# Prologue order of a Perceiver layer kernel: small weights and last rows moved into step 0

## The reference

```python
x = x + xattn(layernorm(x), ctx)     # x 64x32x256, ctx 64x257x256
x = x + attn(layernorm(x))
x = x + ffn(layernorm(x))

def xattn(x, y):
    Q = x @ Wq + bq;  K = y @ Wk + bk;  V = y @ Wv + bv
    K_hat = cos(K @ Wr + br)
    return softmax(Q @ K_hat.T) @ V

def attn(x):                          # causal, the 8 most similar earlier tokens
    score = where(top8(x @ x.T), (x @ W_q.T) @ (x @ W_k.T).T / sqrt(32), -1e9)
    msg = softmax(score) @ x
    mix = sigmoid(log_mix);  scale = softplus(log_scale) + 0.01
    return gelu((mix * x + (1 - mix) * msg) * gain + bias) * scale

def ffn(x):                           # one of 8 experts per token, 256 -> 1024 -> 256
    return p_max * (gelu(x @ W1[e] + b1[e]) @ W2[e] + b2[e])
```

## Time and profile before

| | us |
|---|---|
| median of 3 runs | 526.98 (525.98 to 528.96) |
| profiled execution, its own time | 528.04 |
| profiled execution, span of the trace | 526.1 |
| PE busy in the span | 458.0 (87%) |
| DVE, ACT, POOL busy | 272.8, 267.9, 206.6 |

### The profile page before, as it was taken

How to read it: one execution, slowest core, us unless ns; L and a number is a source line. 1 busy time by engine, 2 the same in 40 slices (tenths; PEclk the granted TensorE clock), 3 DMA queues, 4 the chain that set the end, 5 groups by cost and what they waited for, 6 DMA issues and landing times. The chain is left out here.

```text
span 526.1 us, 10389 instructions
## 1 busy us (share of the span) xinstructions
PE 458.0 (87%) x2848; PEld 339.0 (64%) x2849; DVE 272.8 (52%) x794; ACT 267.9 (51%) x580; POOL 206.6 (39%) x377
## 2 busy tenths in 40 slices
PE   4889999999999889999997632169999999999992
PEld 3555555666666456666564421169999999999991
DVE  1456878778787578778776546501222221222110
ACT  2267668877788578777785331023332233322230
POOL 2441235334453155243532210643544455445331
PEclk9999999999999999999997655569999999999997
DMA  8602521435314333263340012466557555566110
GB/s 229 204 30 91 171 91 44 148 112 191 111 50 143 112 107 102 90 190 110 111 162 20 20 41 101 145 234 220 191 209 212 210 162 182 200 219 208 47 21 0
DMA packets 47880, 68.93 MB, mean 131 GB/s; under 512 B 5469, under 2 KB 39839, under 8 KB 47713
## 3 DMA queue, kind: packets, MB, share of 16 engines
q1 hardware_dynamic: 41808, 59.09, 33.9%
q0 software_dynamic: 3312, 8.13, 5.7%
q10 hardware_dynamic: 2720, 1.26, 0.9%
HBM read 62.17 MB, written 7.21 MB: 132 GB/s over the span
## 5 line engine op out<-in xcount | busy, mean ns | idle before, releaser
L1177 PE MATMUL pK<-stage,Wkr 128*128 128x512 f32 x256 | 124.3, 611 | 2.6 <-DVE stage L674 2.0
L340 POOL TENSOR_SCALAR ve<-mv 128x1 f32<-128x1 f32 x48 | 13.7, 286 | 185.5 <-DVE mv L597 185.5
L1369 PE MATMUL b<-W,XF 128*128 x368 | 83.1, 379 | 0.0
L1369 PEld LDWEIGHTS b<-W,XF 128*128 128x128 f32 x368 | 68.2, 190 | 8.4
L1177 PEld LDWEIGHTS pK<-stage,Wkr 128*128 128x128 f32 x256 | 44.5, 193 | 43.0 <-issue 41.7
L964 DVE SCALAR_TENSOR_TENSOR XF<-b,p_slot,XF 128x256 f32<-128x256 f32 x23 | 11.1, 484 | 104.6 <-PE b L1369 104.6
L1015 ACT ACTIVATE stage<-pK,bkr 128x512 f32<-128x512 f32 x64 | 42.8, 689 | 38.1 <-PE pK L1177 38.1
L1110 ACT ACTIVATE XF<-pT,b_now 128x128 f32<-128x128 f32 x96 | 27.3, 370 | 54.4 <-PE pT L1351 54.3
L1110 ACT ACTIVATE XF<-pK,b_now 128x128 f32<-128x128 f32 x88 | 25.2, 369 | 50.6 <-PE pK L1351 50.6
L1022 ACT ACTIVATE stage<-stage 128x512 f32<-128x512 f32 x64 | 40.5, 633 | 14.9 <-DVE stage L669 14.7
L1351 PE MATMUL pT<-XF,stage 128*128 128x128 f32 x384 | 46.6, 282 | 0.0
(11 more groups left out here) (204 smaller groups left out, 762.2 us busy)
## 6 DMA issues: line engine op xcount, KB each, us to landing
stage<-in_L_ffn_W_dram SPq DMA_DIRECT2D x23, 1024.0 KB
stage<-in_ctx_dram SPq DMA_DIRECT2D x32, 512.0 KB, 4.9
W<-in_L_ffn_W_dram SPq DMA_DIRECT2D x8, 1024.0 KB, 6.0
ctx_last<-in_ctx_dram SPq DMA_DIRECT2D x64, 32.0 KB, 3.9
normal_tokens<-xn SPq DMA_DIRECT2D x16, 128.0 KB, 2.9
residual_tokens<-X SPq DMA_DIRECT2D x16, 128.0 KB, 2.7
X<-in_x_dram SPq DMA_DIRECT2D x1, 1792.0 KB, 7.5
stage<-in_L_ffn_b_dram SPq DMA_DIRECT2D x1, 1024.0 KB, 6.6
```

Source lines behind the costliest of these rows:

```text
L1177: mm = pe.matmul(pK[r][:], Wkr[:, c, r * P:(r + 1) * P], ctx_T[:, c, half * 512:(half + 1) * 512], start=c == 0, stop=c == DC - 1)
L1369: mm = pe.matmul(p_out[b], f_hT[b][:, n * P:(n + 1) * P], W2[:, bass.ds(e, 1), n, :].rearrange("p o d -> p (o d)"), start=n == 0, stop=n = ...
```

## The change

- SP: Wr gets a semaphore of its own, `wr_ld`. ACT: bk and br count on `bk_ld`, and the two logs are issued ahead of x and Wqk.
- PE: the first transposes wait for Wk alone. The key bias moves behind the first context transposes of step 0, the transposes of Wqk and of the last rows (now in b7) behind the second projection, the projection of the last rows (now in b4) behind the second half's context transposes. The three waits ahead of step 0 go; a wait for `wkr_cp` stands ahead of the first projection.
- DVE: the scalars come ahead of step 0; the key bias follows the copy of xnT, the two copies stand ahead of `whole(0, 0)`, the operations of the last rows ahead of `whole(0, 2)`.
- ACT: the wait for `bkr_cp` moves ahead of the first `turn`, and the Sin of the last rows behind the last `sine` of step 0.
- POOL: in step 0 it waits for `khat_last` at the end of the step, copies the column, and makes the masks; the gains move to the end of step 1.

```diff
@@ POOL
-            def late_constants():
+            def gains():
                 pool.wait_ge(S["scal_dve"], 3)
                 (gain_msg, gain_self)
+                pool.wait_ge(S["gains"], 2)
+            def masks():
                 (causal, pickable, unpicked)
...
-                if now:
+                first = isinstance(k, int) and 2 * k + parity == 0
+                def last_key():
                     g, b, _ = now
-                    if isinstance(g, int) and g == 0:
-                        pool.wait_ge(S["khat_last_r"], 1)
...
+                if now and not first:
+                    last_key()
...
-                if isinstance(k, int) and 2 * k + parity == 0:
-                    late_constants()
+                if first:
+                    pool.wait_ge(S["khat_last_r"], 1)
+                    last_key()
+                    masks()
+                if isinstance(k, int) and 2 * k + parity == 1:
+                    gains()
@@ DVE
-            (key bias, copies of WqkT and last_T, last rows' turns and fraction)
             normal_x(0, 0)
+            scalars()
...
                     v.tensor_copy(xnT[:].rearrange("p c n -> p (c n)"), p_xnT).then_inc(S["xnT_cp"], 1)
+                    if isinstance(g, int) and g == 0:
+                        key_bias()
...
                 if now:
+                    if isinstance(now[0], int) and now[0] == 0:
+                        early_copies()
                     whole(now[0], 0)
...
                 if now:
+                    if isinstance(now[0], int) and now[0] == 0:
+                        last_keys()
                     whole(now[0], 2)
@@ ACT
-            act.dma_start(bk[:], ...).then_inc(S["wk_ld"], 16)
-            act.dma_start(br[:], ...).then_inc(S["wk_ld"], 16)
+            act.dma_start(bk[:], ...).then_inc(S["bk_ld"], 16)
+            act.dma_start(br[:], ...).then_inc(S["bk_ld"], 16)
+            act.dma_start(logs[:, 0:1], a["L0_attn_log_mix"].partition_broadcast(P)).then_inc(S["logs_ld"], 16)
+            act.dma_start(logs[:, 1:2], a["L0_attn_log_scale"].partition_broadcast(P)).then_inc(S["logs_ld"], 16)
             act.dma_start(X[:, 0:2, :], x_v[:, 0:2, :]).then_inc(S["x_ld"], 16)
...
-            act.wait_ge(S["bkr_cp"], 1)
...
                 if now:
+                    if isinstance(now[0], int) and now[0] == 0:
+                        act.wait_ge(S["bkr_cp"], 1)
                     turn(now[0], 0)
...
                     sine(g, b, 3)
+                    if isinstance(g, int) and g == 0:
+                        last_keys()
@@ PE
-            pe.wait_ge(S["wk_ld"], 64)
+            pe.wait_ge(S["wk_ld"], 16)
...
+            pe.wait_ge(S["wr_ld"], 16)
...
-            pe.wait_ge(S["bkr_cp"], 1)
-            pe.wait_ge(S["wqkT_cp"], 1)
-            pe.wait_ge(S["last_turn"], 2)
...
                     ctx_transposes(g, b, q, 0)
+                    if first:
+                        key_bias()
...
+                if first:
+                    pe.wait_ge(S["wkr_cp"], 1)
                 if now:
                     ctx_project(now[0], 0, 0)
...
                     ctx_project(now[0], 0, 1)
+                if first:
+                    early_transposes()
...
                     ctx_transposes(g, b, q, 1)
+                if first:
+                    last_keys()
```

More of the change, by code:

```diff
@@ new lines, in scalars @@
+            def scalars():
+                v.wait_ge(S["scal_act"], 1)
+                v.tensor_scalar(sc[:, 1:2], sc[:, 0:1], 1.0, None, ALU.add).then_inc(S["scal_dve"], 1)
+                v.wait_ge(S["scal_dve"], 1)
+                v.reciprocal(sc[:, 2:3], sc[:, 1:2]).then_inc(S["scal_dve"], 1)
+                v.wait_ge(S["scal_dve"], 2)
+                v.tensor_scalar(sc[:, 3:4], sc[:, 2:3], -1.0, 1.0, ALU.mult, ALU.add).then_inc(S["scal_dve"], 1)
+                v.tensor_scalar(sc[:, 8:9], logs[:, 1:2], 0.0, 0.01, ALU.max, ALU.add).then_inc(S["scal_dve"], 1)
+                v.wait_ge(S["scal_act"], 4)
+                v.wait_ge(S["scal_dve"], 4)
+                v.tensor_tensor(sc[:, 9:10], sc[:, 7:8], sc[:, 8:9], ALU.add).then_inc(S["scal_dve"], 1)
+                v.wait_ge(S["scal_dve"], 5)
@@ L992, in _, with last_keys, scalars @@
             act.dma_start(Wroute[:], rows(a["L0_ffn_Wr"])).then_inc(S["w_ld"], 16)
[L995 to L1003, removed]
+            def last_keys():
+                act.wait_ge(S["last_fr"], 1)
+                act.activation(khat_last[:], last_frac, ACT.Sin, scale=TWO_PI).then_inc(S["khat_last_r"], 1)
+            def scalars():
+                act.wait_ge(S["logs_ld"], 2 * 16)
+                act.activation(sc[:, 0:1], logs[:, 0:1], ACT.Exp, scale=-1.0).then_inc(S["scal_act"], 1)
+                act.activation(sc[:, 5:6], logs[:, 1:2], ACT.Abs).then_inc(S["scal_act"], 1)
+                act.wait_ge(S["scal_act"], 2)
+                act.activation(sc[:, 6:7], sc[:, 5:6], ACT.Exp, scale=-1.0).then_inc(S["scal_act"], 1)
+                act.wait_ge(S["scal_act"], 3)
+                act.activation(sc[:, 7:8], sc[:, 6:7], ACT.Ln, bias=1.0).then_inc(S["scal_act"], 1)
+            scalars()
             def ctx_T_copy(g, half):
@@ L1136, in _ @@
             mm.then_inc(S["wkr_mm"], 1)
[L1137 to L1145, removed]
@@ L1146, in _ @@
-            pe.wait_ge(S["last_ld"], 16)
-            for c in range(DC):
-                transposed(b7[:, c * B:(c + 1) * B], last_rows[:, c * P:(c + 1) * P],
-                           "lastT_tr" if c == DC - 1 else None)
-            pe.wait_ge(S["wkr_cp"], 1)
-            pe.wait_ge(S["lastT_cp"], 1)
-            for r in range(DC):
-                for c in range(DC):
-                    mm = pe.matmul(b6[:, r * B:(r + 1) * B], Wkr[:, c, r * P:(r + 1) * P], last_T[:, c, :],
-                                   start=c == 0, stop=c == DC - 1)
@@ L1156, in _, with key_bias @@
-            mm.then_inc(S["lastK_mm"], 1)
-            pe.wait_ge(S["bkr_cp"], 1)
-            pe.wait_ge(S["wqkT_cp"], 1)
-            pe.wait_ge(S["last_turn"], 2)
+            def key_bias():
+                pe.wait_ge(S["bk_ld"], 2 * 16)
+                for r in range(DC):
+                    for ec in range(DC):
+                        mm = pe.matmul(b4[:, r:r + 1], Wr[:, ec, r * P:(r + 1) * P], bk[:, ec:ec + 1],
+                                       start=ec == 0, stop=ec == DC - 1)
+                mm.then_inc(S["bkr_mm"], 1)
@@ new lines, in early_transposes @@
+            def early_transposes():
+                pe.wait_ge(S["wqk_ld"], 32)
+                for c in range(DC):
+                    transposed(b7[:, c * 2 * H:(c + 1) * 2 * H], Wqk[:, c * P:(c + 1) * P],
+                               "wqkT_tr" if c == DC - 1 else None)
+                pe.wait_ge(S["last_ld"], 16)
+                for c in range(DC):
+                    transposed(b7[:, P + c * B:P + (c + 1) * B], last_rows[:, c * P:(c + 1) * P],
+                               "lastT_tr" if c == DC - 1 else None)
@@ L1162, in ctx_transposes, with last_keys @@
+            def last_keys():
+                pe.wait_ge(S["lastT_cp"], 1)
+                pe.wait_ge(S["bkr_sum"], 1)
+                for r in range(DC):
+                    for c in range(DC):
+                        mm = pe.matmul(b4[:, P + r * B:P + (r + 1) * B], Wkr[:, c, r * P:(r + 1) * P], last_T[:, c, :],
+                                       start=c == 0, stop=c == DC - 1)
+                mm.then_inc(S["lastK_mm"], 1)
             def ctx_transposes(g, b, q, half):
@@ L1225, in step @@
                     pe.wait_ge(S["hT_cp"], g + 1)
+                    if isinstance(g, int) and g == 0:
+                        pe.wait_ge(S["wqkT_cp"], 1)
                     at_least(pe, S["xnT_cp"], upto(g + 3, NG))
```

62 lines of the change are left out of this document (26 added, 36 removed).

## The result

The changed kernel is slower, by a little. Its median is 530.51 us (529.27 to 531.26, ten runs), beside 527.81 (525.98 to 529.32, ten runs) of the kernel before: a ratio of 1.0049, with a 95% interval of 1.0030 to 1.0068. The forecast was 524.8 with a range of 522.8 to 526.9. The profiled execution of after has 530.77 with a span of 529.0, where before had 528.04 and 526.1.

The account below looks back on a forecast made before the run. PE was taken as the bound, busy 15.57 of 15.65 us of a step. A gain of 5.35 less 1.4 less 1.75 gave 2.2 us off the median of 526.98: 524.8 us, range 522.8 to 526.9.

Parts of the forecast that it names:

- the load of x costs nothing: Prologue: x behind the two logs lands up to 2 us later, at 10.6, but is wanted only at 14.3.
- nothing past step 1 is touched: Later steps: PE bounds each, so a saving ahead of step 3 reaches the end whole; 2.2 us forecast.
- part 1: Prologue up to the first key projection: it starts at 14.9 and not 20.25, a gain of 5.35 us.
- part 2: Step 0, work moved behind the second projection: third projection at 23.6, 3.95 earlier than before, a cost of 1.4 us.
- part 3: After the last sine of step 0: POOL's later masks delay L1245 of step 1, a cost of 1.75 us.
- PE's start, the context load, the biases: Prologue: PE starts at 4.7, the second context load lands at 10.7, the key bias ends at 14.3.
- The moved work: Step 0: small transposes and last rows' projection on PE behind the second projection; third projection at 23.6.
- T: The time in step 0 when the second projection has been issued, forecast at 20.2.
- The table load: ACT's load of the Sin set in step 0: 1.28 us; the skill page's dearer switch, 1.35 longer, had chance 0.03.
- The masks: POOL's masks take 4.65 us (bounds 4.4 to 5.4), delaying rstd(2), DVE's copy of the probabilities and L1245 in step 1.
- Rival (a): Prologue: PE's clock rises early, about 11, first projection at 13.8; 1.7 us more gained, 523.1; chance 0.14.
- Rival (c): Ahead of the scores: PE's clock falls after 2.05 us idle, costing 1.5 to 3.5 us; 524.9 to 526.9; chance 0.17.

Follow-up runs that it names:

- e7: Changed kernel with the load of x issued ahead of the two logs in ACT's queue; 528.24 us, ratio 1.0018 to the kernel before.
- e11: Changed kernel with eight more fulfilled waits on DVE in step 1 and x loaded ahead of the logs; 521.42 us, ratio 0.9867 to the kernel before.
- e3: Changed kernel with POOL's masks ahead of its wait for khat_last in step 0; 529.64 us, ratio 1.0032 to the kernel before.
- e2: Changed kernel with two fulfilled waits on constants left out on DVE in stats_x of groups 3 and 4; 529.03 us, ratio 1.0025 to the kernel before.
- e5: Changed kernel with eight more fulfilled waits on DVE in step 1; 524.82 us, ratio 0.9951 to the kernel before.
- e6: Kernel before with eight more fulfilled waits on DVE in step 1; 522.39 us, ratio 0.9918 to the kernel before.
- e9: Kernel before with four more fulfilled waits on DVE in step 1; 530.13 us, ratio 1.0037 to the kernel before.
- e4: Changed kernel with two more fulfilled waits on DVE in step 1; 529.82 us, ratio 1.0051 to the kernel before.
- e10: Changed kernel with eight more fulfilled DVE waits and POOL's masks ahead of its wait for khat_last; 523.21 us, ratio 0.9898 to the kernel before.
- e8: Changed kernel with x ahead of the logs, POOL's gains and masks ahead of its khat_last wait, and eight more DVE waits; 520.53 us, ratio 0.9883.
- e12: Changed kernel with eight more fulfilled DVE waits and POOL's masks and gains in step 0 ahead of its khat_last wait; 523.06 us, ratio 0.9888.
- e1: Kernel before with two more fulfilled waits on DVE in step 1; 528.52 us, ratio 1.0019 to the kernel before.

## Why the prediction was wrong, step by step

Two steps failed: that the load of x costs nothing, and that nothing past step 1 is touched. In the profiled pair the sum of the prediction reads so: part 1 gained 3.79 and not 5.35, part 2 cost 1.75 and not 1.4, part 3 cost 1.72 and not 1.75, which leaves 0.3 at the scores of step 3 where 2.2 was forecast; another 2.2 were lost from there to step 11, and 1.1 behind the last scores.

**PE's start, the context load, the biases.** Right: 4.48 (forecast 4.7), transposes at 11.45 (10.7, the load 0.75 late).

**x costs nothing.** Wrong, and the costliest term of part 1. I let two issues push x by 2 us to 10.6 and gave 2 us of cover; it landed at 12.6, 3.9 later than before. I had counted the time of the issues and not what two such transfers do to the one behind them. The text named up to 1 us for x 2 us later still; it was 1.56 in after (16.46 against 14.9), and e7 and e11 show that it was x.

**The moved work.** Nearly right: the third projection followed T (22.18) by 3.36, forecast 3.4, and the first two projections took 5.7 and not 5.3. The table load took 1.28, and its ACTIVATE began 0.06 behind its end, in ACT's rows of after:

```profile
22.99 1.28 ACT L1057 ACT_TABLE_LOAD   x1
24.33 0.63 ACT L1057 ACTIVATE stage<-stage 128x512 f32<-128x512 f32 x1
```

So the drain of 1.38 us in the Trainium skill, "ScalarE: Activation LUTs", What ACT_TABLE_LOAD costs, doesn't show here either.

**The masks.** The mechanism was right and e3 shows it: DVE waits for POOL's `rstd(2)` with POOL in the masks. From the scores to L1300 it was 6.38, forecast 6.9; the masks took 4.4, my lower bound, and not 4.65. Over the whole step the size was right all the same (The rest, below). L1300 stood at 38.72 and not at 37.35.

**The gain of this part itself.** It was read against one profile of before, whose first projection came at 20.25. Two of four profiles of that prologue have it 1.6 to 1.8 earlier. Rival (a), an early rise of the clock, was weighed for the kernel after alone and given 0.14, because the matmuls of 8.4 to 12.0 "didn't raise it before"; they do, in some executions. In after the clock did rise early, at 10.5, but fell again at 13.9; with x in time, e11 has the first projection at 13.70, where rival (a) has 13.8. By the means of four profiles each, the changed prologue gains nothing at L1245 (39.35 against 38.9) and is 0.9 behind at the scores of step 3, since its step 1 is 1.25 to 1.7 longer. That agrees with e2, 0.25% above before with its loop in the same place, and with e5 against e6, where both loops are in a good place: ratios of 0.9951 and 0.9918 and medians 2.4 us apart.

**"A saving ahead of it reaches the end whole; the change touches nothing past step 1."** This step failed worst. The change touches the length of DVE's code, and so the place of the loop. In the profiled pair the scores of step 3 were 0.3 ahead, and 2.2 were lost from there to step 11: 0.5 in steps 3 to 9 and 1.6 in step 10. e9 gives the unchanged order the same halt and the same lower clock (ratio 1.0037), e2 brings the split halt back into the changed kernel. I had the row before my eyes: 181.83 with its 2.05 us of idle time in the earlier trace rows is the halt. I used it to say that the clock survives such a stretch, and never asked why PE idles in the middle of a loop in which a window of 15.65 us else holds 15.57 of PE's work.

**The fall of the clock.** Rival (c) had the right mechanism at the wrong place. A stretch of 2.05 us ahead of the scores left the clock up in after and e5, but the projections behind it ran slow in e7 and e4 (5.40 for the eight records that else take 3.70). Behind 4.1 to 4.3 us it fell in all five profiles that have such a stretch, in after, e4 and e9 for 3.4 us, which at half the rate is a price of 1.7, and in e3 and e7 for 6.8. (The window of 0.55 in the earlier trace rows is 2.7 us at the lower level and not the 3 that the text takes from it.)

**The rest.** From L1300 to step 3 the changed kernel lost another 0.6: the third projection of step 1 came only 0.3 earlier than before (41.55 against 41.85), with DVE's whole and fraction at 0.84 and 0.85 us beside POOL's gains, where they else take 0.42 and 0.69. The masks account for nearly all of it: with them moved (e3, e10) step 1 is within 0.1 of the 14.47 of before, though the gains stay where they are, and moving the gains as well (e8, e12) gives that 0.1. From the last scores to the end, after took 1.1 us more than before; but over the fourteen profiles this part spans 244.4 to 246.3, both ends in kernels with the changed prologue (e3 and e5), so I count it as variation.

## What to carry to other kernels

Before a saving is passed on through a loop, account for every idle stretch in it: the one that ended in "issue" at this loop's jump came with transfers of instructions, and an edit of a few instructions ahead of the loop split it, joined it or ended it. It is worth trying a few idle instructions ahead of a loop on their own account (here 4.3 us, 0.8%, where the reordering at its best, e8 against e6, gave 0.35%), and only then comparing orders of work, each with its loop in the same place. A prologue is to be read from more than one profile, and a tiny load issued ahead of a large one can cost far more than its issue.

## What the hardware showed

- **Halts of DVE at a jump back, with code fetched beside them.** In the kernels with two halts apart they took 2.6 to 2.7 and 1.6 to 1.7 us, with 8 KB transfers of kind "instruction" beside them; a loop that started ahead of record 634 halted twice, one that started at 634 or later not at all. The Trainium skill, "Runtime: NRT & Kernel Launch", Instruction fetch mechanics, says that a taken branch whose target is outside the window held forces a fetch before execution goes on; the halts agree with that. It puts the refill at 16 KiB. Here the transfers beside these halts are of 8 KB, while another queue (q8) has others of 16 KB; the trace doesn't say whose they are, so what holds for DVE is the 8 KB measured beside its halts.
- **The clock around idle PE.** After 4.1 to 4.3 us without work it was at the lower level in every profile (five), for 3.4 or 6.8 us; after 2.0 to 2.2 us it was sometimes so (e2, e4, e7) and sometimes not (before, after, e1 and e5 among others).
- **Two executions of the same prologue can differ by 1.8 us** at the first projection, with a rise of the clock at 12.3 us in one (e6; 11.8 in e9) and none before 23.9 us in the other (before).
- **Small loads ahead of a large one:** two of 0.5 KB ahead of 256 KB, in the same queue, moved its landing from 8.6 to 12.6 us; with the order turned round it was 8.5 again.
